# A two-layer transformer kernel: the score operands of the second attention go through a DRAM scratch, and its output is summed before the projection

## The chip, the cores and the metric

The kernel runs on one core of a Trainium2 chip. The core has a matrix engine (TensorE, PE in the profile, with its weight loads shown apart as PEld), a vector engine (DVE), an activation engine (ScalarE, ACT), GpSimd (POOL) and SyncE (SP), whose queue here issues the DMAs. All of them run their own instruction lists in order and wait for one another by semaphores. The metric is the device time of one execution in microseconds.

## What is computed

Two layers. Each normalises its input x, computes an attention s and a gate g = silu(a feed-forward product), and returns x + s * g. The change is in the second layer: its attention has 16 heads of 16 dimensions over sequences of 256 tokens, 8 sequences (batches), and its feed-forward part is a mixture of experts.

```python
def _L1_attn_ref(x, w_qkv, q_norm_w, k_norm_w, w_proj, b_proj):
    qkv = jnp.einsum('bld,ed->ble', x, w_qkv)
    qkv = qkv.reshape(B, L, 3, H, D).transpose(2, 0, 3, 1, 4)
    q, k, v = (qkv[0], qkv[1], qkv[2])
    q = rmsnorm(q, q_norm_w)
    k = rmsnorm(k, k_norm_w)
    scores = jnp.einsum('bhqd,bhkd->bhqk', q, k) * scale
    attn = jax.nn.softmax(scores, axis=-1)
    out = jnp.einsum('bhqk,bhkd->bhqd', attn, v)
    out = out.transpose(0, 2, 1, 3).reshape(B, L, dim)
    return jnp.einsum('bld,ed->ble', out, w_proj) + b_proj
...
x = x + s * g
xn = _layernorm(x, axis=-1)
s = _L1_attn_ref(xn, ...)
g = _silu(_L1_ffn_ref(xn, ...))
return x + s * g
```

All of it is fp32. PE multiplies in a faster format that keeps fewer bits (fp32r), so every operand is split into a hi part (its rounding) and a lo part (the rest), and a product is three: hi x hi, hi x lo, lo x hi (`product`, lines 58 to 60).

## The kernel before

The first layer takes the time to about 890 us. The second is one merged loop, `stage_layer1`, over slots n = -16 to 132, one head per slot: head u of batch b is slot n = 16 b + u. In slot n PE issues the scores of head n + 1, then the items that a planner has put into the slot, then the turn (four transposes of the normalised probabilities) of head n - 1, then the values product of head n - 2. Around it go, for each head: DVE's row maximum (`l_nb`), ACT's exponentials with their sums (`l_pr`), DVE's reciprocal (`l_ri`), GpSimd's normalisation (`l_pr` again), the turn on PE, and its hi part on ACT and lo part on DVE (both `s_wh`). There is one bank for scores, so the scores of a head wait until the exponentials of the head before have been read out of it.

The items are the attention's own jobs, fixed to slots by `attn_jobs`, and the expert work in pieces: `g`, `G`, `u`, `U` (three matmuls of 512 columns each, gate and up products of an expert tile K, 56 tiles in all) and `D0`, `D1` (six of 256 columns, the down product). The planner goes through the slots with a credit: each slot gets SLOT_GOAL - UNIT units, an item costs the units of COST, and expert pieces are added while there is credit. So fewer units for attention jobs, or a higher goal, put expert pieces into earlier slots, and the table alone sets PE's order. The other engines' orders follow from the same table.

The attention's jobs for a batch: Q0, Q1, V (the products of normalised rows and weights), T (transposes), then the S jobs, one in every second slot, eight per batch, one for a pair of heads. The operands of the scores are stacks: for each head 4 x 16 rows, so that hi and lo parts of q stand against hi and lo parts of k in one product over K = 128 rows (two heads, the query operand `zq` being zero for the other head). The stacks are made with tokens on the partitions (`stq`, `stk`), by ACT (`k_hi`, `q_hi`), GpSimd (`q_lo`) and DVE (`k_lo`), 32 instructions of each. An S job turns them on PE (four transposes), and ACT copies them out of PSUM into `zq` and `sk`, three copies.

The values product of four heads fills one bank with 128 rows: per head 16 rows from the hi part of v and 16 from the lo part. After four heads ACT copies the bank (`out_hi`) and DVE takes the rest (`out_lo`), so `ot` has four blocks of 128 rows, in which hi and lo rows stand side by side, and the projection jobs P0, P1 sum them by multiplying over 4 x 128 rows, 12 matmuls of 256 columns.

SP's queue loads the experts' weights (`l_wd`, `s_wl` from wgu_scratch) and the combine rows (`l_cb`, the experts' weights per token, spread over partitions), each as soon as a buffer comes free, in a loop over K.

## Time and profile before

| | us |
|---|---|
| median of 3 runs (lowest, highest) | 1409.71 (1409.17, 1410.26) |
| profiled execution | 1408.91 |
| its span, first to last instruction | 1407.1 |
| busy in the span: PE, DVE, ACT, POOL | 1368.9, 920.9, 820.0, 761.9 |

Busy time is a union of an engine's instructions; matmuls are pipelined, so their listed durations overlap and the step between two starts is the better measure of what one costs. The stage that the change touches is the last third of the span.

### The profile page before, as it was taken

To read this page: it belongs to the slowest core of one execution; us is meant where nothing else is said; L and a number is where in the kernel's file an instruction comes from. 1 tells how busy PE (TensorE), PEld (TensorE's weight loads), DVE (VectorE), ACT (ScalarE), POOL (GpSimd) and SP (SyncE) were. 2 spreads that over 40 slices of the span, in tenths; PEclk is the share of its full clock that TensorE was granted. 3 is DMA by queue.
4 is the path that set the end of the run, shared out by engine and by line. 5 is a ranking of instruction groups with operands and counts; after the bars stand their busy time and mean duration, and the time that the engine had idled before them with its cause. 6 is when DMAs were issued, how large, how long until landed. Compare 5 with 4: busy or idle time off the path is not lost. (4 is left out here: it accounts for less than half of the span.)

```text
span 1407.1 us, 25856 instructions
## 1 busy us (share of the span) xinstructions
PE 1368.9 (97%) x8950; PEld 1221.1 (87%) x8950; DVE 920.9 (65%) x1793; ACT 820.0 (58%) x2172; POOL 761.9 (54%) x757
## 2 busy tenths in 40 slices
PE   9999899999999999999999999899999999999997
PEld 7887798999899989998999888788889888889887
DVE  6655566565656565656665665677777878777764
ACT  5553444554544555445544544378787788778873
POOL 2651433454434454435544443477669677777764
PEclk9999999999999999999999999999999999999999
DMA  5995333334332343223433334144233242342442
GB/s 197 323 330 198 85 91 89 92 80 120 100 94 52 101 130 99 75 75 98 114 86 94 113 75 165 68 122 150 83 98 123 68 150 84 120 120 92 143 122 90
DMA packets 85681, 165.64 MB, mean 118 GB/s; under 512 B 16720, under 2 KB 27664, under 8 KB 83248
## 3 DMA queue, kind: packets, MB, share of 16 engines
q1 hardware_dynamic: 85552, 163.99, 38.3%
q8 instruction: 73, 1.20, 0.4%
q14 instruction: 56, 0.46, 0.1%
HBM read 99.90 MB, written 22.09 MB: 87 GB/s over the span
## 5 line engine op out<-in xcount | busy, mean ns | idle before, releaser
L775 POOL TENSOR_TENSOR a_pr<-a_pr,a_ri 128x512 f32<-128x512 f32 x128 | 133.5, 1043 | 299.1 <-DVE a_ri L955 299.1
L832 ACT ACTIVATE a_pr<-a_score,a_nb 128x256 f32<-128x256 f32 x256 | 119.3, 471 | 266.3 <-DVE a_nb L947 266.3
L1337 POOL TENSOR_TENSOR l_pr<-l_pr,l_ri 128x512 f32<-128x512 f32 x128 | 133.5, 1043 | 119.0 <-DVE l_ri L1714 118.1
L1465 ACT ACTIVATE l_pr<-l_score,l_nb 128x256 f32<-128x256 f32 x256 | 119.2, 472 | 80.8 <-DVE l_nb L1680 80.2
L58 PE MATMUL a_job<-s_xs,s_wh 128*128 128x512 f32 x384 | 153.9, 401 | 1.0 <-PEq L221 1.0
L60 PE MATMUL a_job<-s_xs,s_wl 128*128 128x512 f32 x384 | 151.7, 395 | 0.0
L59 PE MATMUL a_job<-s_xs,s_wh 128*128 128x512 f32 x384 | 151.3, 394 | 0.0
L947 DVE TENSOR_REDUCE a_nb<-a_score 128x2 f32<-128x512 f32 x128 | 88.5, 692 | 85.0 <-PE a_score L1026 83.3
L1680 DVE TENSOR_REDUCE l_nb<-l_score 128x2 f32<-128x512 f32 x128 | 87.5, 684 | 34.0 <-PE l_score L1820 33.4
L960 DVE TENSOR_TENSOR a_pt<-a_turn,a_pt 128x512 fp32r<-128x512 f32 x128 | 87.5, 683 | 24.2 <-ACT a_pt L840 24.2
L1844 PE MATMUL l_out<-s_wh,l_vp 128*128 128x256 f32 x512 | 91.6, 300 | 0.9 <-DVE s_wh L1684 0.9
L58 PE MATMUL l_job<-l_xs,s_wl 128*128 128x512 f32 x224 | 90.6, 405 | 1.7 <-DVE l_ga L1594 1.7
L1684 DVE TENSOR_TENSOR s_wh<-l_turn,s_wh 128x512 fp32r<-128x512 f32 x128 | 87.2, 681 | 5.5 <-ACT s_wh L1473 5.4
L1473 ACT ACTIVATE s_wh<-l_turn 128x512 fp32r<-128x512 f32 x128 | 76.5, 597 | 23.4 <-PE l_turn L1830 23.0
L60 PE MATMUL l_job<-l_xs,s_wl 128*128 128x512 f32 x224 | 88.9, 397 | 0.0
L59 PE MATMUL l_job<-l_xs,s_wl 128*128 128x512 f32 x224 | 88.6, 396 | 0.0
L955 DVE RECIPROCAL a_ri<-a_sm 128x2 f32<-128x2 f32 x128 | 21.2, 166 | 102.3 <-ACT a_pr L832 102.3
L1830 PE MATMUL l_turn<-s_ident,l_pr 128*128 128x128 f32 x512 | 77.9, 275 | 10.5 <-DVE s_wh L1684 9.4
L60 PEld LDWEIGHTS a_job<-s_xs,s_wl 128*128 128x128 f32 x384 | 72.1, 188 | 16.9
L1830 PEld LDWEIGHTS l_turn<-s_ident,l_pr 128*128 128x128 f32 x512 | 59.3, 140 | 28.6 <-issue 13.6
L844 ACT ACTIVATE a_ot<-a_out 128x512 fp32r<-128x512 f32 x64 | 38.8, 606 | 77.8 <-PE a_out L60 76.8
L58 PEld LDWEIGHTS a_job<-s_xs,s_wh 128*128 128x128 f32 x384 | 72.2, 188 | 11.3 <-issue 1.4
(257 smaller groups left out, 4780.3 us busy)
## 6 DMA issues: line engine op xcount, KB each, us to landing
s_wl<-wgu_scratch SPq DMA_DIRECT2D x56, 512.0 KB, 4.8
a_sk<-a_rotk SPq DMA_DIRECT2D x384, 64.0 KB, 2.0
a_sq<-a_rotq SPq DMA_DIRECT2D x256, 64.0 KB, 2.0
s_xs<-xn_scratch SPq DMA_DIRECT2D x14, 1024.0 KB, 5.6
l_wd<-wd_scratch SPq DMA_DIRECT2D x56, 256.0 KB, 2.7
a_raw<-in_w SPq DMA_DIRECT2D x30, 256.0 KB, 3.0
wgu_scratch<-f_split SPq DMA_DIRECT2D x14, 512.0 KB, 4.7
f_praw<-in_moe_w SPq DMA_DIRECT2D x14, 384.0 KB, 4.5
```

What stands on the lines that cost most here:

```text
L58: pe.matmul(out, lh, rh, start=first, stop=False)
L59: pe.matmul(out, lh, rl, start=False, stop=False)
L60: return pe.matmul(out, ll, rh, start=False, stop=last)
L775: pool.tensor_tensor(e, e, ri[:, n % 2, :].unsqueeze(2).broadcast_to([P, 2, SEQ]), ALU.mult)\
L832: i = act.activation(pr[:, n % 2, t, :], PS[n % 2][:, t * SEQ:(t + 1) * SEQ], ACT.Exp, bias=nb[:, n % 2, t:t + 1], accum_out=sm[:, n % 2, ...
L947: dve.tensor_reduce(nb[:, (n + 1) % 2, :], PS[(n + 1) % 2][:, :].rearrange("p (t k) -> p t k", t=2), AX.X, ALU.max, negate=True).then_inc( ...
L960: dve.tensor_tensor(pt[:, n % 2, 1, :], PT[:, :], pt[:, n % 2, 0, :], ALU.subtract).then_inc(S["turn_free"], 1)
L1337: pool.tensor_tensor(e, e, ri[:, n % 3, :].unsqueeze(2).broadcast_to([P, 2, SEQ]), ALU.mult)\
L1465: i = act.activation(pr[:, n % 3, t, :], PS[n % NPS][:, t * SEQ:(t + 1) * SEQ], ACT.Exp, bias=nb[:, n % 3, t:t + 1], accum_out=sm[:, n % 3 ...
L1680: dve.tensor_reduce(nb[:, (n + 1) % 3, :], PS[(n + 1) % NPS][:, :].rearrange("p (t k) -> p t k", t=2), AX.X, ALU.max, negate=True).then_in ...
L1830: i = pe.transpose(PT[:, kc * SEQ + t * P:kc * SEQ + (t + 1) * P], pr[:, n % 3, t, kc * P:(kc + 1) * P], ident[:, :])
L1844: i = pe.matmul(PO[:, 0:SEQ], vp[:, kc, a, e * P:(e + 1) * P], pt[:, n % 2, q, kc * SEQ:(kc + 1) * SEQ], start=(e == 0 and kc == 0 and q = ...
```

## The change

It does four things, all in the second layer.

- The normalised rows of q and k of a batch are turned once, in two X jobs of four transposes each (in slots u = 9 and 11 of the batch before; batch 0 in slots -7 and -5). ACT copies the hi part of the turned rows out of PSUM (`tqk`), DVE takes the lo part. `k_hi`, `q_hi`, `q_lo`, `k_lo` and the S jobs with their evictions go.
- SP writes the turned rows to DRAM scratches in the order of the stacks, eight DMAs for each X job (`store_stack`, in slots u = 10 and 12), and reads the stacks of a pair of heads back into `zq` and `sk` with three DMAs (`load_stack`, in every odd slot, four slots ahead of the pair's first scores). The scores wait for these loads. SP's loop now runs over slots, and a load of expert data stands in the slot in which its buffer comes free.
- The rows of v are laid out so that the hi parts of four heads fill one half of the bank and the lo parts the other. ACT copies the lo half across to the partitions of the hi half (`out_low`), DVE adds the two (`out_sum`). After eight heads ACT and DVE split the 128 summed rows into hi and lo parts (`out_hi`, `out_lo`), and the projection runs over 2 x 128 rows.
- The planner's cost of a P job goes from 12 to 6 units and SLOT_GOAL from 30.6 to 28.35.

The rest of the diff renames semaphores, makes the weights of the projection two blocks instead of four, and adds the scratches.

```diff
-VG, VSTRIDE, VBLK = 4, 160, 640
+VG, VB, VSTRIDE, VBLK = 4, 2, 144, 576
+VHALF = VG * D1
...
-    T, Q, V, S_, P_, LOG, CMB, GU, DH = 4, 12, 12, 4, 12, 20, 4, 12, 6
+    T, Q, V, S_, P_, LOG, CMB, GU, DH = 4, 12, 12, 4, 6, 20, 4, 12, 6
...
-    UNIT, SLOT_GOAL, EARLY_GOAL = 10, 30.6, 14
+    UNIT, SLOT_GOAL, EARLY_GOAL = 10, 28.35, 14
...
-        m, r = divmod(n + 4, H1)
-        if r % 2 == 0 and 0 <= m < BATCH:
-            jobs.append((f"S{r // 2}", m))
+        if b + 1 < BATCH and u in (9, 11):
+            jobs.append((f"X{u // 2 - 4}", b + 1))
...
+                def store_stack(m, half):
+                    wait_free(sp, (f"X{half}", m))
+                    heads = slice(8 * half, 8 * half + 8)
+                    for part, to, places in ((0, qs_dram, ((0, 2), (1, 3))), (1, ks_dram, ((0, 1), (2, 3)))):
+                        for low in range(2):
+                            for place in places[low]:
+                                sp.dma_start(to[m % 2, heads, place], tqk[:, half, low, part, :].bitcast(F32)).then_inc(tqk_out[half], 16)
+
+                def load_stack(pair):
+                    m, p = divmod(pair, H1 // 2)
+                    r = pair % NSTK
+                    if p % 4 == 0:
+                        sp.wait_ge(tqk_out[p // 4], 16 * 8 * (m + 1))
+                    if pair >= NSTK:
+                        sp.wait_ge(S["score_full"], 2 * (pair - NSTK) + 2)
+                    for h in range(2):
+                        sp.dma_start(zq[64 * h:64 * h + 64, r, h, :].bitcast(F32),
+                                     qs_dram[m % 2, 2 * p + h].rearrange("c d n -> (c d) n")).then_inc(zq_in[r], 16)
+                    sp.dma_start(sk[:, r, :].bitcast(F32), ks_dram[m % 2, 2 * p:2 * p + 2].rearrange("h c d n -> (h c d) n")).then_inc(sk_in[r], 16)
...
+                for n in SLOTS:
+                    b, u = divmod(n, H1)
+                    if b + 1 < BATCH and u in (10, 12):
+                        store_stack(b + 1, u // 2 - 5)
+                    pair = (n + 5) // 2
+                    if n % 2 and 0 <= pair < N // 2:
+                        load_stack(pair)
+                    for K in LOAD_AT[n]:
+                        load_experts(K)
+                    for K in range(2, L):
+                        if LOAD_GU[K] == n:
+                            load_gu(K)
...
-                    elif name[0] == "S":
...
-                        for h in range(2):
-                            act.activation(zq[64 * h:64 * h + 64, r, h, :], bank[64 * h:64 * h + 64, 0:SEQ], ACT.Copy)
-                        act.activation(sk[:, r, :], bank[:, SEQ:2 * SEQ], ACT.Copy).then_inc(free_of(item), 1)
+                    elif name[0] == "X":
+                        half = int(name[1])
                         wait_full(act, item)
+                        if m >= 1:
+                            act.wait_ge(tqk_out[half], 16 * 8 * m)
+                        act.activation(tqk[:, half, 0].rearrange("p r n -> p (r n)"), bank[:, :], ACT.Copy).then_inc(S["turned_hi"], 1)
...
-                def out_hi(g):
+                def out_low(g):
+                    here, there = VHALF * (g % 2), VHALF * (1 - g % 2)
                     act.wait_ge(S["pv_done"], 4 * g + 4)
...
+                    act.activation(ol[here:here + VHALF, :], PO[there:there + VHALF, 0:SEQ], ACT.Copy).then_inc(S["out_low"], 1)
+
+                def out_hi(k):
+                    act.wait_ge(S["out_free"], 2 * k + 2)
+                    if k >= VB:
+                        wait_full(act, ("P1", k // VB - 1))
+                    act.activation(ot[:, 0, k % VB, :], os[:, k % VB, :], ACT.Copy).then_inc(S["out_hi"], 1)
...
-                def out_lo(g):
-                    dve.wait_ge(S["out_hi"], g + 1)
-                    dve.tensor_tensor(ot[:, 1, g % VG, :], PO[:, 0:SEQ], ot[:, 0, g % VG, :], ALU.subtract).then_inc(S["out_free"], 1)
+                def out_sum(g):
+                    here = VHALF * (g % 2)
+                    dve.wait_ge(S["out_low"], g + 1)
+                    if g >= 4:
+                        dve.wait_ge(S["out_lo"], (g - 4) // 2 + 1)
+                    dve.tensor_tensor(os[here:here + VHALF, g // 2 % VB, :], PO[here:here + VHALF, 0:SEQ], ol[here:here + VHALF, :], ALU.add)\
+                       .then_inc(S["out_free"], 1)
+
+                def out_lo(k):
+                    dve.wait_ge(S["out_hi"], k + 1)
+                    dve.tensor_tensor(ot[:, 1, k % VB, :], os[:, k % VB, :], ot[:, 0, k % VB, :], ALU.subtract).then_inc(S["out_lo"], 1)
...
-                        pe.wait_ge(S["out_free"], VG * (m + 1))
-                        for a in range(VG):
+                        pe.wait_ge(S["out_lo"], VB * (m + 1))
+                        for a in range(VB):
...
                     if u % 2 == 0:
-                        wait_free(pe, (f"S{u // 2}", m))
+                        pe.wait_ge(zq_in[r], 16 * 2 * (n // 2 // NSTK + 1))
+                        pe.wait_ge(sk_in[r], 16 * (n // 2 // NSTK + 1))
```

Three places in the orders of instructions. First PE: a slot of before with an S job, from the scores on (L1820 are the scores, L58 to L60 an expert piece, L1773 the S job, L1742 to L1744 a down piece).

```order
L1820 MATMUL l_score<-l_sk,l_zq 128x256 x2
L58 MATMUL l_job<-l_xs,s_wl 128x512
L59 MATMUL l_job<-l_xs,s_wl 128x512
L60 MATMUL l_job<-l_xs,s_wl 128x512
L1773 MATMUL l_job<-s_ident,l_stq 128x128 x2
L1773 MATMUL l_job<-s_ident,l_stk 128x128 x2
L1742 MATMUL l_down<-l_wd,l_hid 128x256
L1743 MATMUL l_down<-l_wd,l_hid 128x256
L1744 MATMUL l_down<-l_wd,l_hid 128x256
L1742 MATMUL l_down<-l_wd,l_hid 128x256
L1743 MATMUL l_down<-l_wd,l_hid 128x256
L1744 MATMUL l_down<-l_wd,l_hid 128x256
```

In the changed kernel the slot that has the X1 job of the same batch, to the next slot's scores (L1787 is the X job, L59 to L61 an expert piece, L1844 the turn, L1858 the values).

```order
L1834 MATMUL l_score<-l_sk,l_zq 128x256 x2
L1787 MATMUL l_job<-s_ident,l_qk 128x128 x4
L59 MATMUL l_job<-l_xs,s_wl 128x512
L60 MATMUL l_job<-l_xs,s_wl 128x512
L61 MATMUL l_job<-l_xs,s_wl 128x512
L59 MATMUL l_job<-l_xs,s_wl 128x512
L60 MATMUL l_job<-l_xs,s_wl 128x512
L61 MATMUL l_job<-l_xs,s_wl 128x512
L1844 MATMUL l_turn<-s_ident,l_pr 128x128 x4
L1858 MATMUL l_out<-s_wh,l_vp 128x256 x4
L1834 MATMUL l_score<-l_sk,l_zq 128x256 x2
```

The four transposes now read the rows themselves (`l_qk`) and stand in two slots of sixteen; the slots between have scores, expert pieces, turn and values alone.

Second SP's queue, before, in the middle of a batch (L1242 and L1247 are the weights of an expert tile, L1262 the combine rows).

```order
L1242 DMA s_wl<-wgu_scratch 128x1024
L1247 DMA l_wd<-wd_scratch 128x512
L1262 DMA l_cb<-ct_scratch 64x512 x2
L1242 DMA s_wl<-wgu_scratch 128x1024
L1247 DMA l_wd<-wd_scratch 128x512
L1262 DMA l_cb<-ct_scratch 112x512
L1262 DMA l_cb<-ct_scratch 16x512
L1242 DMA s_wl<-wgu_scratch 128x1024
```

In the changed kernel, slots u = 9 to 12 of a batch (L1272 are the stores, L1282 and L1284 the loads of a pair's stacks, L1243, L1248, L1263 the loads of before).

```order
L1263 DMA l_cb<-ct_scratch 64x512 x2
L1243 DMA s_wl<-wgu_scratch 128x1024
L1272 DMA qs_scratch<-l_tqk 8x16x256 x4
L1272 DMA ks_scratch<-l_tqk 8x16x256 x4
L1282 DMA l_zq<-qs_scratch 64x256 x2
L1284 DMA l_sk<-ks_scratch 128x256
L1243 DMA s_wl<-wgu_scratch 128x1024
L1272 DMA qs_scratch<-l_tqk 8x16x256 x4
L1272 DMA ks_scratch<-l_tqk 8x16x256 x4
L1248 DMA l_wd<-wd_scratch 128x512
L1263 DMA l_cb<-ct_scratch 112x512
L1263 DMA l_cb<-ct_scratch 16x512
```

Sixteen stores and a pair's loads have come between the loads of expert weights and combine rows.

Third DVE in the slot u = 2 after a batch's first: before, the last low part of the attention's output stands right behind the low part of the turn (L1680 is a row maximum, L1684 the low part of a turn, L1655 `out_lo`, L1602 to L1605 row norms, L1714 the reciprocal).

```order
L1680 TENSOR_REDUCE l_nb<-l_score 128x2
L1684 TENSOR_TENSOR s_wh<-l_turn,s_wh 128x512
L1655 TENSOR_TENSOR l_ot<-l_out,l_ot 128x256
L1602 TENSOR_REDUCE l_ss<-l_sqr 128x64
L1603 TENSOR_SCALAR l_ss<-l_ss 128x64
L1605 TENSOR_SCALAR l_rq<-l_ss 128x64
L1598 TENSOR_TENSOR l_ga<-l_ga,l_job 128x512
L1714 RECIPROCAL l_ri<-l_sm 128x2
```

In the changed kernel the sum `out_sum` (L1664) has that place, and `out_lo` (L1669) stands behind the row norms and the reciprocal (L1726), two places ahead of the next row maximum (L1694).

```order
L1694 TENSOR_REDUCE l_nb<-l_score 128x2
L1698 TENSOR_TENSOR s_wh<-l_turn,s_wh 128x512
L1664 TENSOR_TENSOR l_os<-l_out,l_ol 64x256
L1614 TENSOR_REDUCE l_ss<-l_sqr 128x64
L1615 TENSOR_SCALAR l_ss<-l_ss 128x64
L1617 TENSOR_SCALAR l_rq<-l_ss 128x64
L1726 RECIPROCAL l_ri<-l_sm 128x2
L1669 TENSOR_TENSOR l_ot<-l_os,l_ot 128x256
L1610 TENSOR_TENSOR l_ga<-l_ga,l_job 128x512
```

So the operand of the projection jobs, which PE has in the slots u = 3 and 4, is finished later in DVE's slot.

## Rows read from the trace of the kernel before

**Rows 1.** The page, busy time of each engine over the span.

```profile
PE 1368.9 (97%) x8950; PEld 1221.1 (87%) x8950; DVE 920.9 (65%) x1793; ACT 820.0 (58%) x2172; POOL 761.9 (54%) x757
```

**Rows 2.** Stretches of time: length, busy time of each engine, granted clock, DMA.

```profile
core 0: us, PE busy (x) PEld busy (x) DVE busy (x) ACT busy (x) POOL busy (x), PEclk, DMA share, GB/s
...
921.60:1383.80 462.20, 449.02 (x3137) 404.40 (x3138) 349.34 (x739) 358.79 (x1051) 339.75 (x414) 1.00 0.37 115
1000.30:1051.40 51.10, 46.76 (x314) 41.38 (x313) 40.79 (x92) 40.49 (x117) 31.18 (x34) 1.00 0.28 89
1250.50:1303.40 52.90, 52.90 (x377) 48.27 (x377) 36.72 (x74) 43.23 (x127) 39.84 (x52) 1.00 0.38 121
```

**Rows 3.** Waits of the second layer: total us, times, longest.

```profile
ACT l_pr L1465 <- DVE l_nb L1680: 80.2, 106, 2.1
...
PE l_turn L1830 <- DVE s_wh L1684: 9.4, 14, 1.3
...
PEld l_turn L1830 <- POOL l_pr L1337: 7.6, 9, 1.7
```

**Rows 4.** Timeline of PE, two neighbouring slots: start us, us, instruction.

```profile
1261.14 0.39 PE L1820 MATMUL l_score<-l_sk,l_zq 128*128 128x256 f32 x2
...
1262.06 0.38 PE L1773 MATMUL l_job<-s_ident,l_stq 128*128 128x128 f32 x2
...
1264.80 0.40 PE L1820 MATMUL l_score<-l_sk,l_zq 128*128 128x256 f32 x2
...
1265.74 0.28 PE L1742 MATMUL l_down<-l_wd,l_hid 128*128 128x256 f32 x1
...
1266.32 0.28 PE L1744 MATMUL l_down<-l_wd,l_hid 128*128 128x256 f32 x1
...
1268.04 0.28 PE L1820 MATMUL l_score<-l_sk,l_zq 128*128 128x256 f32 x1
```

**Rows 5.** Groups by shape: count, busy us, mean ns, idle before.

```profile
L1420 ACT ACTIVATE l_zq<-l_job 64x256 fp32r<-64x256 f32 x128 | 48.0, 375 | 1.5 <-PE l_job L1773 0.5
...
L1773 PE MATMUL l_job<-s_ident,l_stk 128*128 128x128 f32 x128 | 24.4, 272 | 0.0
...
L1619 DVE TENSOR_TENSOR l_stk<-l_qk,l_stk 128x256 fp32r<-128x256 f32 x32 | 23.1, 762 | 0.0
...
L58 PE MATMUL l_job<-s_wl,l_ot 128*128 128x256 f32 x64 | 18.4, 287 | 0.0
...
L1655 DVE TENSOR_TENSOR l_ot<-l_out,l_ot 128x256 fp32r<-128x256 f32 x32 | 13.2, 414 | 1.2 <-ACT l_ot L1479 1.2
```

**Rows 6.** Timeline of one slot at 1019 us, rows of DVE, ACT, PE.

```profile
1020.77 0.73 DVE L1582 SCALAR_TENSOR_TENSOR l_ga<-l_gt,l_gz 128x512 f32<-128x512 f32 x1 [2.57 <-ACT l_gt L1439]
...
1021.09 0.74 ACT L1449 ACTIVATE l_stk<-l_qk 128x256 fp32r<-128x256 f32 x2
...
1022.85 0.63 PE L1830 MATMUL l_turn<-s_ident,l_pr 128*128 128x128 f32 x4 [0.84 <-DVE s_wh L1684]
```

**Rows 7.** Timeline of SP's queue in the first layer, loads of 64 KB.

```profile
418.46 3.70 SPq L689 DMA_DIRECT2D a_sk<-a_rotk  x6
```

**Rows 8.** The page, DMA issues: count, KB each, us to landing.

```profile
a_sk<-a_rotk SPq DMA_DIRECT2D x384, 64.0 KB, 2.0
...
l_wd<-wd_scratch SPq DMA_DIRECT2D x56, 256.0 KB, 2.7
```

**Rows 9.** Stores to a DRAM scratch: issue ns, shortest, median and longest.

```profile
L249 SPq DMA_DIRECT2D xn_scratch<-s_xs x4: 339/876/1222, 12.8 to 94.4; - x4
```

**Rows 10.** Two stretches at the head of the second layer, columns of rows 2.

```profile
897.00:900.20 3.20, 3.05 (x26) 3.08 (x27) 2.70 (x6) 0.00 (x0) 2.14 (x5) 0.99 0.00 0
900.20:903.60 3.40, 3.40 (x11) 2.75 (x10) 2.80 (x12) 0.88 (x3) 2.52 (x8) 0.50 0.00 0
```

**Rows 11.** Timeline of the head, rows of POOL, SP and PE.

```profile
911.54 1.66 POOL L1317 TENSOR_TENSOR l_stq<-l_qk,l_stq 128x256 fp32r<-128x256 f32 x2 [0.18 <-ACT l_stq L1457]
...
918.35 0.36 SPq L1262 DMA_DIRECT2D l_cb<-ct_scratch  x1
...
918.69 0.39 PE L1820 MATMUL l_score<-l_sk,l_zq 128*128 128x256 f32 x2
...
922.86 1.30 POOL L1344 TENSOR_TENSOR l_ga<-l_ga,l_cb 128x512 f32<-128x512 f32 x1
```

More of the change, by code:

```diff
@@ L750, in _ @@
                     sp.dma_start(l1.w[:, :, c].bitcast(F32), w1_dram[c]).then_inc(l1.w_in, 16)
-                for i in range(2):
-                    sp.dma_start(l1.wp[:, :, 2 * i:2 * i + 2].bitcast(F32).rearrange("p s a d -> p s (a d)"), wp_dram[i]).then_inc(l1.w_in, 16)
+                sp.dma_start(l1.wp.bitcast(F32).rearrange("p s a d -> p s (a d)"), wp_dram[0]).then_inc(l1.w_in, 16)
                 sp.wait_ge(S["job_full"], JOB["k3", NST - 1] + 1)
@@ L1077, in _, with stage_layer1 @@
                 rest(PS[(N - 2) % 2], 9)
-def stage_layer1(nc, sh, l1, wgu_dram, wd_dram, ct_dram, out):
+def stage_layer1(nc, sh, l1, wgu_dram, wd_dram, ct_dram, qs_dram, ks_dram, out):
     N = BATCH * H1
@@ L1133, in stage_layer1 @@
     JOB = {item: i for i, item in enumerate(ORDER)}
+    LOAD_SLOT, at = {}, SLOTS[0]
+    for K in range(L + 1):
+        s, k = divmod(K, MT)
+        at = max(at, AT["D1", K - 1 - ND] if K > ND else SLOTS[0], AT["C", s] if k == NSH + 1 and s < NSTEP else SLOTS[0])
+        LOAD_SLOT[K] = at
+    LOAD_GU = {K: AT["U", K - NGU] if K >= NGU else SLOTS[0] for K in range(L)}
+    LOAD_AT = {n: [K for K in LOAD_SLOT if LOAD_SLOT[K] == n] for n in SLOTS}
     U_AT = {n: [K for K in range(L) if AT["U", K] == n] for n in SLOTS}
@@ L1196, in stage_layer1 @@
         gu_in = l1.gu_in
+        zq_in, sk_in = ([n_.sem(f"{s}_in{i}") for i in range(NSTK)] for s in ("zq", "sk"))
+        tqk_out = [n_.sem(f"tqk_out{i}") for i in range(2)]
         d_in, cb_in = ([n_.sem(f"{s}_in{i}") for i in range(3)] for s in ("d", "cb"))
@@ L1223, in tokens @@
             return slice(at, at + P)
-        def heads(t, part, half):
-            at = part * D + half * P
-            return qk[:, t, at:at + P].rearrange("p (h d) -> p h d", d=D1).unsqueeze(2).broadcast_to([P, 8, 2, D1])
-        def half_of(rows, t, half):
-            return rows[:, t, 8 * half:8 * half + 8]
         def wait_merged(engine, s):
@@ L1272, in store, with load_experts @@
                                      x1[:, s * TT + 2 * i:s * TT + 2 * i + 2, :]).then_inc(S["stored"], 16)
-                for K in range(L + 1):
-                    if 2 <= K < L:
-                        load_gu(K)
+                def load_experts(K):
                     if K >= 1:
@@ L1313, in weigh @@
                         .then_inc(S["weighted"], 1)
-                def q_lo(m, half, t):
-                    pool.wait_ge(S["q_hi"], 4 * m + 2 * half + t + 1)
-                    pool.tensor_tensor(half_of(stq, t, half)[:, :, 1::2, :].bitcast(F32R), heads(t, 0, half),
-                                       half_of(stq, t, half)[:, :, 0::2, :], ALU.subtract).then_inc(S["q_lo"], 1)
                 def spread(m, a):
@@ L1442, in job_out @@
                             act.activation(gt[:, m % 2, :], bank[:, :], ACT.Tanh, scale=0.5).then_inc(S["tanh_ready"], 1)
-                def k_hi(m, half):
-                    act.wait_ge(S["scaled"], m + 1)
-                    if m >= 1:
-                        wait_full(act, (f"S{4 * half + 3}", m - 1))
-                    for t in range(TB):
-                        act.activation(half_of(stk, t, half)[:, :, 0:2, :].bitcast(F32R), heads(t, 1, half), ACT.Copy)\
-                           .then_inc(S["k_hi"], 1)
-                def q_hi(m, half):
-                    act.wait_ge(S["weighted"], m + 1)
-                    if m >= 1:
-                        wait_full(act, (f"S{4 * half + 3}", m - 1))
-                    for t in range(TB):
-                        act.activation(half_of(stq, t, half)[:, :, 0::2, :].bitcast(F32R), heads(t, 0, half), ACT.Copy)\
-                           .then_inc(S["q_hi"], 1)
                 def exps(n):
@@ L1614, in scale_rows @@
                                       rq[:, :].unsqueeze(2).broadcast_to([P, 4 * H1, D1]), ALU.mult).then_inc(S["scaled"], 1)
-                def k_lo(m, half):
-                    for t in range(TB):
-                        dve.wait_ge(S["k_hi"], 4 * m + 2 * half + t + 1)
-                        dve.tensor_tensor(half_of(stk, t, half)[:, :, 2:4, :].bitcast(F32R), heads(t, 1, half),
-                                          half_of(stk, t, half)[:, :, 0:2, :], ALU.subtract).then_inc(S["k_lo"], 1)
                 def rows(ap):
@@ L1714, in _ @@
                         dve.reciprocal(ri[:, (n + 1) % 3, :], sm[:, (n + 1) % 3, :]).then_inc(S["sum_inv"], 1)
+                    if n >= 10 and (n - 10) % 8 == 0 and (n - 10) // 8 < VB * BATCH:
+                        out_lo((n - 10) // 8)
                     for item in second:
@@ L1851, in _ @@
                 do_item(("T", 0))
-                pe.wait_ge(l1.w_in, 64)
+                pe.wait_ge(l1.w_in, 48)
                 rest(PO, 5)
@@ L1877, in program @@
     ct = nc.dram_tensor("ct_scratch", [2, E, STEP], F32, kind="Internal").ap()
+    qs = nc.dram_tensor("qs_scratch", [2, H1, 4, D1, SEQ], F32, kind="Internal").ap()
+    ks = nc.dram_tensor("ks_scratch", [2, H1, 4, D1, SEQ], F32, kind="Internal").ap()
     with ExitStack() as ctx:
@@ L1884, in program @@
             stage_attention0(nc, a, sh, s0, l1, xn0, g0, w1, wp, wgu)
-        stage_layer1(nc, sh, l1, wgu, wd, ct, out)
+        stage_layer1(nc, sh, l1, wgu, wd, ct, qs, ks, out)
 def tile_weights(gate, up, down):
@@ L1901, in proj_rows @@
     import numpy as np
-    rows = [[(VG * a + p // (2 * D1)) * D1 + p % D1 for p in range(P)] for a in range(VG)]
+    rows = [[(2 * VG * j + p // D1) * D1 + p % D1 for p in range(P)] for j in range(VB)]
     return np.concatenate([w[r] for r in rows], axis=1)
```

64 lines of the change are left out of this document (27 added, 37 removed).

## Prediction

> **What bounds the kernel now.** I read the busy line of the page first: PE works in 97% of the span, DVE in 65%, ACT in 58% [rows 1]. That is an average over two layers, and the change is in the second one, so the next view was the busy time by stretches. From 921.6 to 1383.8 us, where 126 heads run with the experts' products between them, PE is busy 449.0 of 462.2 us at the full granted clock, DVE 349.3 and ACT 358.8 [rows 2]. So 13.2 us of that stretch are not PE's own work, and they are not spread evenly: from 1250.5 to 1303.4 PE has no idle time at all, from 1000.3 to 1051.4 it has 4.3 us [rows 2]. The third view is the waits. The long one (ACT's exponential behind DVE's row maximum, 80.2 us) is ACT's idle time and costs nothing while PE goes on; PE's own largest is its turn of the probabilities behind DVE's low part of the head before, 9.4 us in 14 times [rows 3]. The reader should see: work taken from PE here is nearly all time, work taken from ACT is time only in the few slots where a chain over ACT and DVE ends last.
>
> The timeline of two neighbouring slots shows what an instruction is worth on PE. A slot with an S job takes from 1261.14 to 1264.80, 3.66 us; the next one, alike but without it, to 1268.04, 3.24 us [rows 4]. So an S job (four fp32 transposes) costs 0.42 us. Six matmuls of 256 columns start 0.116 us apart (1265.74 to 1266.32 over five steps) [rows 4]; their listed durations of 0.28 overlap and are not to be added.
>
> **Removed from PE.** 64 S jobs become 16 X jobs of four transposes each: 48 x 0.42 = 20.2 us. The projection multiplies over 2 blocks of 128 rows rather than 4, so 6 of 12 matmuls go in each of 16 P jobs: the three lines hold 64 matmuls each [rows 5], 192, of which 96 go: 96 x 0.116 = 11.1 us. Together 31.3 us, all in the second layer. The values, turns, scores and expert products stay. The planner's goal falls from 30.6 to 28.35 units, so expert pieces move to earlier slots to fill the room; that is what turns the saving into shorter slots (most come to 3.24 us [rows 4]) instead of gaps, and itself costs nothing.
>
> **The other engines.** ACT loses the evictions of S (48.0 us, and half as much for the sk tile) and the hi copies into the stacks; it gains 32 low-half copies of 64x256 at about 0.375 us, the price of the same shape in the S eviction [rows 5], 12 us, and 16 X copies of 128x512. DVE loses 32 low parts of k at 0.762 us mean (24.4 us) and gains 16 X subtractions, at most twice the 0.414 us of a subtraction of half the size from PSUM [rows 5], 13 us, and per eight heads one operation more, 16 x 0.41 = 7 us. So DVE's sum falls a little, ACT's much, and GpSimd loses its low parts of q. No engine but PE is near the span by its sum. I price these edits at nothing on the sum, because PE's 449 us cover them. Without that cover, where the chain decides, they are a gain: in the slot at 1019 PE waited 0.84 us for DVE, whose work of that slot began after 2.57 us of waiting for ACT, and ACT put 0.74 us of k's hi copies between [rows 6]. Those copies go.
>
> One new low part is unlike the old: out_lo now reads two SBUF tiles, where the old one read PSUM. The traces show that kind of difference: k's low part from two SBUF tiles takes 0.762 us on average, the old out_lo of equal size from PSUM 0.414 [rows 5]. So 16 out_lo may take 0.35 us more, 6 us of DVE time that PE covers, against 32 of the slow kind that go. The Trainium skill, page "SBUF — State Buffer", section "Who interferes with whom", says that a DVE instruction with two SBUF inputs and a GpSimd instruction reading SBUF shut each other out for a whole instruction; the trace agrees in that mean. By that rule the change halves the exposed instructions; by the row of equal size alone the DVE sum would differ by those 6 us, and the time by nothing.
>
> **Added on the SP queue.** Before each batch SP stores the turned rows in two bursts of eight DMAs of 128 KB, and loads three per pair of heads, 64 pairs. No row shows a store of this shape. Below: 0.34 us of issue, the fastest of four stores to xn_scratch; above: 1.22, the slowest of them [rows 9]. In between, six 64 KB loads took 3.70 us back to back, 0.62 each [rows 7], nearest in kind and size; I take that. A burst is then 5.0 us, a pair's loads 1.9. A pair is loaded four slots (13 us) ahead of its scores, and lands in about 2.0 us [rows 8], so a queue that is one burst late still delivers. Behind the stores in the same queue stand the experts' weights and the combine rows cb. The first cb was issued at 918.35 and used at 922.86, 4.5 us later [rows 11], so a burst in front of it can be felt. GpSimd's combine then runs late, behind it the normalisation of a head, and PE's turn waits for that. From 0 to 1 us a burst, 16 bursts; I take 0.2, 3 us.
>
> **New waits.** P0 waits for out_lo, which now comes behind three operations on row norms and a reciprocal in DVE's slot. Bounds: nothing, and 0.8 us in each of 8 batches; nearer nothing, since PE has scores and expert pieces ahead of it. I take 2 us in all. At the head the first scores stand at 918.69; the change puts X0 where the first q low part ran, at 911.54 to 913.20 [rows 11]. From about 912.5: eight stores of 0.62 us, 2.0 to land, three loads of 0.62, 2.0 to land, give 923.4, 4.7 us late. With 0.34 for each issue it is 920.2, 1.5 us late. I take 3; nothing stands behind PE's wait that could run instead, and if the clock falls over it, as it stood at 0.50 (1.2 of 2.4 GHz) from 900.2 to 903.6 after 3.2 us with only 26 matmuls [rows 10], 1.7 us more, half of those 3.4. The Trainium skill, page "DMA: Bandwidth & Descriptors", section "Why a DMA increments its semaphore by 16 and not by 1", says that the slowest dimension of both sides sets how many of 16 DMA engines share a transfer; with 8 heads in front it would be 8 here. By that the 128 KB would load each engine like 256 KB over all, which lands in 2.7 instead of 2.0 us [rows 8], and the head would be 0.7 us later; no run here shows it yet.
>
> At the end, the last P0 and P1 are short (counted above) but their operand passes four operations instead of two (0.8 us more); PE's keep-busy products cover most of that, and I set it to nothing, plus or minus 1.
>
> **Sum.** Against the profiled execution's 1408.9 us (its span of 1407.1 and 1.8 around it, 0.8 under the median of the runs): 1408.9 - 31.3 + 3 (head) + 3 (SP bursts) + 2 (out_lo) = 1385.6 us. PE's present 13.2 us of waiting are taken to stay: shorter slots leave the chains less cover, but the chains lose ACT and DVE work too.
>
> **Rivals.** (1) The chains shrink with the work: the new waits cost nothing and half of the 13.2 us of idle time goes, since k's hi copies [rows 6] are out of ACT's way: 1408.9 - 31.3 + 3 - 6.6 = 1374. For it: the slot at 1019; against: DVE's sum hardly falls, and its 349 us are a larger share of a shorter stretch (349 of about 433, 81% instead of 76%). (2) The SP bursts and DVE's chain take back more: 0.75 us more in each of 16 bursts, 12 us, gives 1397.6. For it: cb's 4.5 us and a queue without a second one; against: most loads are issued well ahead. (3) Nothing is gained: the slots end at the chains, whatever PE has to do. ACT's 80.2 us behind DVE would be the sign, but there is a stretch of 52.9 us without any idle time of PE [rows 2], so this needs every slot to change its limit: about 1409. (4) Slower: the stores issue at 1.22 us each. Two bursts are then 19.5 us in about four slots (13 us), in which SP also has about 3.7 us of pair loads and 3 of expert loads: it falls 13 us behind, the weights with it, and PE waits some 8 us in each of 7 batches: 1385.6 + 56 = 1442. It decides the sign from 23 / 7 = 3.3 us a batch. Against it: only one row is that long, and the queue stores 1 MB there, not 128 KB.
>
> **How the numbers follow.** A measurement of this kernel can tell about 0.2%, 2.8 us, from no change. The forecast's case, 1380 to 1391, has 0.50; rival 1, down to 1372, 0.20; rival 2, 1391 to 1406, 0.22; rival 3 0.03; rival 4 0.05. Faster 0.92, same 0.03, slower 0.05. With the head at 1.5 and the other two unknown costs at nothing the sum is 1379.1, and only rival 1 lies below; with the head at 6.4, the bursts at 16 and out_lo at 6.4 it is 1406.4. The range from 1374 to 1400 leaves out 0.04 below, about 0.06 of rival 2 and the last two rivals, 0.18 in all.
>
> **What would show it.** In the profile after: S transposes gone, X groups of 16 x 4; the projection lines halved; slots without other jobs at 3.24 us; PE still over 95% busy in the second layer; one wait of some us at the first scores, ended by the sk or zq DMA. Wrong: PE waits at scores for DMAs all along, store issues over 1 us, or the turn's wait for DVE or GpSimd well above 9.4 and 7.6 us [rows 3]; or slots that stay at 3.6 us although PE has 3.24 us of work in them.

## The result, and the profile after

The changed kernel takes 1445.38 us (median of 4 runs, 1444.11 to 1449.18) against 1409.44: the ratio is 1.0252, with an interval from 1.0238 to 1.0266. It is slower by 36 us; the forecast was 1385.6, in a range from 1374 to 1400. The busy line of the page, and the span with its granted clock:

```profile
PE 1351.5 (94%) x8662; PEld 1201.0 (83%) x8662; DVE 915.3 (63%) x1793; ACT 754.9 (52%) x1947; POOL 743.2 (51%) x724
...
core 0: 1444.7 us, clock 0.981
```

Each figure of the busy line is below the one before [rows 1], and the span is 37.6 us longer. By stretches, from the row maximum of the first head to that of the last: 464.4 us before (919.8 to 1384.2), 497.4 after (926.5 to 1423.9). So 33.0 us lie among the heads, 6.7 at the head of the layer, and its tail is 2.1 us shorter. The stretch of the heads, and four pieces of one hole in it (columns of [rows 2]):

```profile
926.50:1423.90 497.40, 433.98 (x2871) 385.48 (x2871) 344.92 (x742) 299.04 (x843) 325.49 (x386) 0.96 0.58 173
...
992.00:996.00 4.00, 0.26 (x3) 0.05 (x1) 0.00 (x0) 0.00 (x0) 0.00 (x0) 0.84 0.82 245
996.00:1000.00 4.00, 0.00 (x0) 0.00 (x0) 0.00 (x0) 1.07 (x3) 2.36 (x3) 0.50 0.94 289
1000.00:1004.00 4.00, 1.88 (x9) 1.92 (x10) 2.56 (x5) 2.15 (x7) 3.53 (x6) 0.50 1.03 293
1004.00:1008.00 4.00, 4.00 (x23) 3.52 (x22) 3.26 (x10) 2.65 (x7) 0.99 (x2) 0.88 0.38 115
```

PE now has 63 us in which it does nothing, where it had 13.2 [rows 2], and its clock falls to the lower level (1.2 of 2.4 GHz) behind a hole. The waits of the layer (total us, times, longest), those of SP's queue last:

```profile
POOL l_ga L1371 <- DMA l_cb<-ct_scratch: 49.4, 10, 11.2
PE l_turn L1844 <- DVE s_wh L1698: 44.4, 29, 9.9
...
PEld l_turn L1844 <- POOL l_pr L1364: 23.1, 23, 2.8
...
PE l_score L1834 <- DMA l_sk<-ks_scratch: 14.0, 3, 8.1
...
SPq L1282 <- DMA ks_scratch<-l_tqk: 22.5, 8, 4.3
```

The wait that was not there before is GpSimd's for the combine rows cb, 49.4 us; the turn's wait for DVE (9.4 before [rows 3]) stands behind it. It and the turn's wait for GpSimd (23.1, before 7.6) are the sign of being wrong that the prediction named. Followed through the hole at 992, SP's queue first (L1272 stores, L1282 and L1284 a pair's loads, L1263 cb):

```profile
974.78 2.51 SPq L1272 DMA_DIRECT2D qs_scratch<-l_tqk  x4
977.34 2.72 SPq L1272 DMA_DIRECT2D ks_scratch<-l_tqk  x4
983.92 1.13 SPq L1282 DMA_DIRECT2D l_zq<-qs_scratch  x2
985.09 0.59 SPq L1284 DMA_DIRECT2D l_sk<-ks_scratch  x1
985.72 0.43 SPq L1243 DMA_DIRECT2D s_wl<-wgu_scratch  x1
986.20 2.52 SPq L1272 DMA_DIRECT2D qs_scratch<-l_tqk  x4
988.75 2.98 SPq L1272 DMA_DIRECT2D ks_scratch<-l_tqk  x4
991.78 0.69 SPq L1248 DMA_DIRECT2D l_wd<-wd_scratch  x1
992.51 1.00 SPq L1263 DMA_DIRECT2D l_cb<-ct_scratch  x2
```

Then GpSimd, which had been free since 986.5, and PE:

```profile
997.64 1.26 POOL L1371 TENSOR_TENSOR l_ga<-l_ga,l_cb 128x512 f32<-128x512 f32 x1 [11.16 <-DMA l_cb<-ct_scratch]
998.86 1.04 POOL L1364 TENSOR_TENSOR l_pr<-l_pr,l_ri 128x512 f32<-128x512 f32 x1
...
1002.12 0.66 PE L1844 MATMUL l_turn<-s_ident,l_pr 128*128 128x128 f32 x2 [9.85 <-DVE s_wh L1698]
```

The two bursts and what stands between them hold SP from 974.78 to 991.78, 17.0 us: stores 5.3, then 3.9 us in which SP itself waits until they have landed, a pair's loads and a weight load 2.2, stores 5.6. The cb rows issue at 992.5, GpSimd has them 5 us later, and PE stands for 9.85 us. Summed over the layer SP is not short of time: it still stands 110.3 us (L1248) and 65.3 us (L1243) until a product frees a weight buffer. It is late by the block, not by the sum. At the head of the layer the same happens twice, before the first and the third head's scores:

```profile
925.66 0.77 PE L1834 MATMUL l_score<-l_sk,l_zq 128*128 128x256 f32 x2 [4.93 <-DMA l_sk<-ks_scratch]
...
940.56 0.76 PE L1834 MATMUL l_score<-l_sk,l_zq 128*128 128x256 f32 x2 [8.11 <-DMA l_sk<-ks_scratch]
```

### The profile page after: what moved, and what is told of

It reads as the page before. It is cut to its first block and busy times, and to the rows that moved or that the text cites. A ratio compares the mean times of both kernels' runs of the same rounds, so it can differ in the third digit from the quotient of the medians.

```text
span 1444.7 us, 25243 instructions
## 1 busy us (share of the span) xinstructions
PE 1351.5 (94%) x8662; PEld 1201.0 (83%) x8662; DVE 915.3 (63%) x1793; ACT 754.9 (52%) x1947; POOL 743.2 (51%) x724
## 5 line engine op out<-in xcount | busy, mean ns | idle before, releaser
L59 PE MATMUL a_job<-s_xs,s_wh 128*128 128x512 f32 x384 | 153.9, 401 | 1.0 <-PEq L222 1.0
L61 PE MATMUL a_job<-s_xs,s_wl 128*128 128x512 f32 x384 | 151.7, 395 | 0.0
L60 PE MATMUL a_job<-s_xs,s_wh 128*128 128x512 f32 x384 | 151.3, 394 | 0.0
L1844 PE MATMUL l_turn<-s_ident,l_pr 128*128 128x128 f32 x512 | 80.0, 280 | 46.9 <-DVE s_wh L1698 44.4
L1844 PEld LDWEIGHTS l_turn<-s_ident,l_pr 128*128 128x128 f32 x512 | 60.0, 143 | 67.0 <-issue 37.1
L1694 DVE TENSOR_REDUCE l_nb<-l_score 128x2 f32<-128x512 f32 x128 | 87.4, 683 | 40.2 <-PE l_score L1834 39.8
L1858 PE MATMUL l_out<-s_wh,l_vp 128*128 128x256 f32 x512 | 93.9, 306 | 0.0
L59 PE MATMUL l_job<-l_xs,s_wl 128*128 128x512 f32 x224 | 90.3, 403 | 2.2 <-DVE l_ga L1606 2.2
L60 PE MATMUL l_job<-l_xs,s_wl 128*128 128x512 f32 x224 | 89.5, 400 | 0.0
L61 PE MATMUL l_job<-l_xs,s_wl 128*128 128x512 f32 x224 | 89.5, 399 | 0.0
L61 PEld LDWEIGHTS a_job<-s_xs,s_wl 128*128 128x128 f32 x384 | 72.1, 188 | 16.9
L1371 POOL TENSOR_TENSOR l_ga<-l_ga,l_cb 128x512 f32<-128x512 f32 x44 | 57.1, 1298 | 51.1 <-DMA l_cb<-ct_scratch 49.4
L59 PEld LDWEIGHTS a_job<-s_xs,s_wh 128*128 128x128 f32 x384 | 72.2, 188 | 11.3 <-issue 1.4
```

Source lines behind the costliest of these rows:

```text
L59: pe.matmul(out, lh, rh, start=first, stop=False)
L60: pe.matmul(out, lh, rl, start=False, stop=False)
L61: return pe.matmul(out, ll, rh, start=False, stop=last)
L1694: dve.tensor_reduce(nb[:, (n + 1) % 3, :], PS[(n + 1) % NPS][:, :].rearrange("p (t k) -> p t k", t=2), AX.X, ALU.max, negate=True).then_in ...
L1844: i = pe.transpose(PT[:, kc * SEQ + t * P:kc * SEQ + (t + 1) * P], pr[:, n % 3, t, kc * P:(kc + 1) * P], ident[:, :])
L1858: i = pe.matmul(PO[:, 0:SEQ], vp[:, kc, a, e * P:(e + 1) * P], pt[:, n % 2, q, kc * SEQ:(kc + 1) * SEQ], start=(e == 0 and kc == 0 and q = ...
```

## The experiments

**The two halves of the change, alone.** The first kept the S jobs and took only the summed output and the short projection; the second the reverse.

```diff
 # projection alone, against the kernel before
-    T, Q, V, S_, P_, LOG, CMB, GU, DH = 4, 12, 12, 4, 12, 20, 4, 12, 6
-    UNIT, SLOT_GOAL, EARLY_GOAL = 10, 30.6, 14
+    T, Q, V, S_, P_, LOG, CMB, GU, DH = 4, 12, 12, 4, 6, 20, 4, 12, 6
+    UNIT, SLOT_GOAL, EARLY_GOAL = 10, 29.85, 14
...
 # stacks alone, against the changed kernel
-    T, Q, V, S_, P_, LOG, CMB, GU, DH = 4, 12, 12, 4, 6, 20, 4, 12, 6
-    UNIT, SLOT_GOAL, EARLY_GOAL = 10, 28.35, 14
+    T, Q, V, S_, P_, LOG, CMB, GU, DH = 4, 12, 12, 4, 12, 20, 4, 12, 6
+    UNIT, SLOT_GOAL, EARLY_GOAL = 10, 29.1, 14
```

> Only the second half of the change: both parts of the attention's output summed on the way out, projection over 256 rows, S jobs and SP's loop as before, the planner's goal at 29.85 units. Queue theory (SP's stores and the wait for them hold up the combine rows cb, and all else follows): this half has no stores, so it gains its 96 matmuls, 11.1 us, about 1399. Rival 'short slots' (the chains over ACT, DVE and GpSimd lose their cover when PE has less to do): a part of the 11.1 us at most, 1403 to 1409. Rival 'traffic': as the queue theory.

> Only the first half: rows turned once, stacks by way of the DRAM scratch, S jobs gone, output and projection as before, goal 29.1. Queue theory: all of the loss is here, and the projection's 11 us are missing: about 1452 to 1460. Rival 'traffic': the same. Rival 'short slots': PE has 11 us more work as cover than in the changed kernel, so no slower than it, 1440 to 1447.

The projection alone gave 1410.21 us, ratio 1.0004 (0.9995 to 1.0014): none of its 11 us. The stacks alone gave 1453.08. So the loss is all in the scratch, as the queue theory had it, but the queue theory was wrong on the other half. The stretch of [rows 2] in the projection's kernel:

```profile
921.60:1383.80 462.20, 439.84 (x3032) 392.93 (x3031) 358.37 (x750) 364.95 (x1062) 343.71 (x412) 1.00 0.37 115
```

PE is busy 9.2 us less than before and idle 9.2 us more; DVE and ACT have 9 and 6 us more. So PE's time was freed where something else ends the slots. Whether that is the work that was there before or the 9 us that DVE now has more, this run does not separate.

**Order in SP's list.** Two kernels moved loads and nothing else.

```diff
 # experts' loads first in each slot
+                    for K in LOAD_AT[n]:
+                        load_experts(K)
...
                     if b + 1 < BATCH and u in (10, 12):
                         store_stack(b + 1, u // 2 - 5)
...
 # cb early: cb leaves load_experts, and has a slot of its own
-                    if K >= 1 and not is_shared(K - 1):
-                        load_cb(K - 1)
+    CB_SLOT = {K: max(LOAD_SLOT[K // MT * MT + NSH + 1], AT["U", ROUTED[j - NCB]] + 2 if j >= NCB else SLOTS[0]) for j, K in enumerate(ROUTED)}
```

> The changed kernel, but in each slot SP issues the experts' loads first, then the stores, then the pair's loads; same DMAs, same bytes. Queue theory: cb loads no longer stand behind a burst of their own slot, the 49 us that GpSimd waits for cb fall to under 20 and the time to 1400 to 1425. Rival 'traffic': no change, 1440 to 1448. Rival 'short slots': no change.

> The changed kernel with the same stores, loads, bytes and buffers, but each cb load stands in SP's list up to two slots earlier, as soon as the combine of three routed tiles before has freed its buffer, instead of behind the weights of its tile. Queue theory with cb as the victim: GpSimd's wait for cb (49 us) falls under 10 and the time to 1400 to 1420. Rival 'pair loads' (the waits for cb only hide that zq, sk or the weights would be as late): cb's wait goes, waits at scores or expert pieces take its place, 1435 to 1447. Rival 'traffic': no change.

The first gave 1452.40 us, a miss: the wait for cb fell only to 35.6 us, and the scores' wait for the stacks rose from 14.0 to 28.8. The experts' loads wait for a product late in PE's slot (SP waits 140.7 us for it, where it was 110.3), and the stores and pairs behind them came later by that. The second gave 1427.69, 17.7 us better with the same transfers, between the ranges of the queue theory and of the rival 'pair loads'. The wait for cb fell to 8.3 us, once, but the rival is half right as well:

```profile
PE l_score L1837 <- DMA l_sk<-ks_scratch: 27.1, 7, 9.9
```

A queue that is 17 us behind makes late whatever stands last in it.

**Fewer stores.** The same bytes in four DMAs of 256 KB (rows of all 8 heads in each, the row order inside a head changed alike for q and k), and then the same with four small stores more.

```diff
-                        for low in range(2):
-                            for place in places[low]:
-                                sp.dma_start(to[m % 2, heads, place], tqk[:, half, low, part, :].bitcast(F32)).then_inc(tqk_out[half], 16)
+                    for i in range(2):
+                        sp.dma_start(qs_dram[m % 2, half, :, i], tqk[:, half, :, 0, :].bitcast(F32)).then_inc(tqk_out[half], 16)
+                    for i in range(2):
+                        sp.dma_start(ks_dram[m % 2, half, :, :, i], tqk[:, half, :, 1, :].bitcast(F32)).then_inc(tqk_out[half], 16)
...
 # and in the second kernel
+                    for i in range(4):
+                        sp.dma_start(small_dram[m % 2, half, i], tqk[:, half, 0, 0, 0:16].bitcast(F32)).then_inc(tqk_out[half], 16)
```

> The changed kernel with the same bytes stored in four DMAs of 256 KB for each X job instead of eight of 128 KB, rows of a head interleaved differently in the scratch, loads of the same sizes. Queue theory: a burst takes 2.4 instead of 5.0 us of SP's issue and its landing starts earlier, so SP is about 6 us less late per batch: 1405 to 1425. Rival 'traffic': same bytes, so 1440 to 1448. Rival 'short slots': no change.

> The kernel with four stores of 256 KB for each X job, and four stores of 8 KB behind them, to a scratch that nobody reads: as many issues as in the changed kernel, the bytes of the version with four. Queue theory by number of issues: 4 x 0.6 us more per burst, so most of the 29 us that the four stores gave back is lost again, 1430 to 1445. Rival 'shape' (the four were better because each large store spreads over more DMA engines and lands sooner): 1416 to 1422.

Four stores: 1416.30 us, 29 us better. With the small ones: 1426.49, 10 of the 29 lost again, less than was expected. SP's queue at the first batch with four stores:

```profile
967.18 0.95 SPq L1269 DMA_DIRECT2D qs_scratch<-l_tqk  x2
968.17 1.96 SPq L1271 DMA_DIRECT2D ks_scratch<-l_tqk  x2
974.53 1.13 SPq L1282 DMA_DIRECT2D l_zq<-qs_scratch  x2
...
976.81 0.94 SPq L1269 DMA_DIRECT2D qs_scratch<-l_tqk  x2
977.80 1.74 SPq L1271 DMA_DIRECT2D ks_scratch<-l_tqk  x2
979.58 0.87 SPq L1248 DMA_DIRECT2D l_wd<-wd_scratch  x1
```

From the first store to the first load behind the second burst it is 12.4 us here against 17.0. The bytes are the same, so traffic as such is not what made the change slow. 64 issues fewer gave 29 us, 64 small ones more took 10. The block tells why the two differ: on average over the eight batches it is 17.3 us long with eight stores, 11.8 with four and 15.2 with the small ones. These cost SP nearly as much issue (0.50 us in the median), but SP waits less for landing (10.3 us in 6 waits, against 22.5 in 8). So the issues and the landing both count. Whether the larger stores also spread over the DMA engines in another way, no run shows.

**Another queue.** The stores from ScalarE's queue, eight or four of them.

```diff
-                                sp.dma_start(to[m % 2, heads, place], tqk[:, half, low, part, :].bitcast(F32)).then_inc(tqk_out[half], 16)
+                                act.dma_start(to[m % 2, heads, place], tqk[:, half, low, part, :].bitcast(F32)).then_inc(tqk_out[half], 16)
...
                     if n in SUM_AT:
                         y_tanh(SUM_AT[n])
+                    if b + 1 < BATCH and u in (10, 12):
+                        store_stack(b + 1, u // 2 - 5)
```

> The changed kernel with its eight stores issued on ScalarE's queue instead of SP's, nothing else. Queue theory: SP's bursts go, but ScalarE stands 5 us in two slots of 16 with the exponentials of the next head behind it: 1395 to 1415. Rival 'traffic' or 'short slots': 1440 to 1448.

> The version with four stores, but issued on ScalarE's queue at the end of its slot, behind the rounding copies. Same DMAs, same bytes; SP's queue has loads alone. Queue theory: SP no longer comes late, cb's wait goes under 8 us and the time to 1388 to 1402; ScalarE pays about 2 us of issue in two slots of 16. Rival 'traffic': as the version with four stores on SP, 1413 to 1420. Rival 'short slots': as well.

Eight: 1473.87 us, four: 1416.61. Both miss. ScalarE's timeline in the kernel with eight:

```profile
981.97 2.47 ACTq L1497 DMA_DIRECT2D qs_scratch<-l_tqk  x4
984.47 3.88 ACTq L1497 DMA_DIRECT2D ks_scratch<-l_tqk  x4
988.74 0.60 ACT L1469 ACTIVATE s_wh<-l_turn 128x512 fp32r<-128x512 f32 x1 [6.18 <-issue]
```

An issue holds the engine that makes it for 0.6 us and more, and ScalarE has the turn of a head behind it, where SP had loads with some slots to spare. The stores are no cheaper there, only worse placed. Nor was SP relieved of them: it stood 75.1 us (eight) and 49.6 us (four) in its own queue until they had landed, where it was 22.5 and 22.2 with the stores in its own list. The four cost the same from either queue (1416.61 and 1416.30).

**Both cures, and what is left.** Four stores and the early cb together; then three variants of it: the row norms of q and k over 4 of 16 elements, the projection's half taken back, and the pairs' loads three slots ahead instead of four.

```diff
 # short norm
-                    own(dve.tensor_reduce(ss[:, :], sqr[:, :, :].rearrange("p t (g d) -> p (t g) d", d=D1), AX.X, ALU.add))
+                    own(dve.tensor_reduce(ss[:, :], sqr[:, :, :].rearrange("p t (g d) -> p (t g) d", d=D1)[:, :, 0:4], AX.X, ALU.add))
...
 # lead of three
-                    pair = (n + 5) // 2
-                    if n % 2 and 0 <= pair < N // 2:
+                    pair = (n + 4) // 2
+                    if n % 2 == 0 and 0 <= pair < N // 2:
```

> Both single cures of the queue together: four stores of 256 KB for each X job, and cb loads as soon as their buffer is free. The four stores alone gave 1416, the early cb alone 1428 from 1445. Queue theory: what is left of the waits for cb (23 us) and at scores (27 us) goes, 1400 to 1408, and no batch of heads has a slot over 8 us except at the head. If the two cure the same microseconds only: 1413 to 1418.

> The version with both cures, and the sum of squares in the row norms of q and k taken over 4 of 16 elements (12 of 16 are left out), which takes about 0.8 us off one DVE instruction in slot 2 of each batch; nothing else changes. Theory 'short slots' (with the queue cured, DVE's order ends the slots 1 to 5 of a batch, since PE has 3.2 us of work there and DVE over 4): 0.5 to 0.8 us in each of 8 batches, 4 to 7 us below the version with both cures. Queue theory alone: no difference over 2 us.

> The version with both cures but with output and projection as in the kernel before (K of 128 rows for four heads, 12 matmuls in a P job, goal 29.1): what the projection's half is worth when the queue does not decide. By PE's work it would be 11 us slower than with it. Theory 'short slots': PE's 11 us lie in slots that DVE ends, so 0 to 6 us slower only.

> The version with both cures, with the loads of a pair three slots ahead of its scores instead of four, and ahead of the stores in a slot, so that SP need not stand still until a batch's first stores have landed (22 us in 7 to 8 waits so far). Queue theory: SP's wait for landing falls under 5 us, the time 2 to 8 us below the version with both cures, unless the shorter lead makes zq and sk late: then waits at scores rise over 10 us and it is slower.

Both cures: 1407.57 us, ratio 0.9989 (0.9980 to 0.9998), within what can be told from the kernel before. GpSimd waits 5.0 us for cb, once, and in five batches (the second, and the fourth to the seventh) no slot is over 5.1 us; these five take some 57 us each all the same, with PE busy in 53 to 54 of them. The short norm gives a part of the reason: 1399.47, 8.1 us less (the runs of either version scatter by 4 us). The norm runs once at the head and in one slot of each of seven batches, and each time it takes 0.80 us less. Of the 9.4 us between the two traced executions, 4.6 are its slots in the second to the seventh batch (0.6 to 0.8 each). 2.4 lie ahead of the first row maximum and 2.1 in the first batch, where the waits at the head move as well. DVE's timeline of the slot in the version with both cures, from one row maximum to the next:

```profile
1174.16 0.67 DVE L1699 TENSOR_REDUCE l_nb<-l_score 128x2 f32<-128x512 f32 x1
1174.74 0.68 DVE L1703 TENSOR_TENSOR s_wh<-l_turn,s_wh 128x512 fp32r<-128x512 f32 x1
1175.45 0.43 DVE L1669 TENSOR_TENSOR l_os<-l_out,l_ol 64x256 f32<-64x256 f32 x1
1175.91 1.22 DVE L1619 TENSOR_REDUCE l_ss<-l_sqr 128x64 f32<-128x1024 f32 x1
...
1177.63 0.75 DVE L1611 SCALAR_TENSOR_TENSOR l_ga<-l_job,s_bias,l_ga 128x512 f32<-128x512 f32 x1
1178.29 0.15 DVE L1731 RECIPROCAL l_ri<-l_sm 128x2 f32<-128x2 f32 x1
1178.37 0.40 DVE L1674 TENSOR_TENSOR l_ot<-l_os,l_ot 128x256 fp32r<-128x256 f32 x1
1178.69 0.68 DVE L1699 TENSOR_REDUCE l_nb<-l_score 128x2 f32<-128x512 f32 x1
```

And with the short norm:

```profile
1167.39 0.67 DVE L1699 TENSOR_REDUCE l_nb<-l_score 128x2 f32<-128x512 f32 x1
...
1169.15 0.42 DVE L1619 TENSOR_REDUCE l_ss<-l_sqr 128x64 f32<-128x256 f32 x1
...
1171.12 0.68 DVE L1699 TENSOR_REDUCE l_nb<-l_score 128x2 f32<-128x512 f32 x1
```

4.53 us, with no idle time shown on DVE, become 3.73: the slot is as long as DVE's list. Taking the projection's half back cost 2.0 us (1409.57) of PE's 11, which fits that. The shorter lead gave 1410.70, no gain: the wait for landing fell from 22.1 to 12.5 us, the waits at scores rose from 10.1 to 12.5.

**The head of the layer, and the clock.** The version with both cures, with the stores of X1 two slots later; and this with 14 filler products ahead of the first scores.

```diff
-                    if b + 1 < BATCH and u in (10, 12):
-                        store_stack(b + 1, u // 2 - 5)
+                    if b + 1 < BATCH and u in (10, 14):
+                        store_stack(b + 1, (u - 10) // 4)
...
 # and in the second kernel
+                    if n == -1:
+                        rest(PO, 14)
```

> The version with both cures (four stores, early cb), with the four stores of X1 two slots later, behind the loads of the next pair. Queue theory: at the head the second pair's loads no longer stand behind these stores and the 10 us between the second and the third head fall to 4 to 6, in the other batches the bursts lie further apart: 1399 to 1405. If the head only waits for DMA latency: 1406 to 1409.

> The same with 14 products of 512 columns (3.2 us, results unused) ahead of PE's first scores, where it stood still for 3.1 us. Clock theory: the granted clock stays at full over the first slots, where it was 0.5 to 0.6 for some 4 us behind that wait, so 1 to 3 us less although PE does more. If the clock falls through something else: no change, or up to 1 us more.

The first: 1401.14 us, ratio 0.9933 (0.9918 to 0.9948), faster than both kernels; the time between the second and the third head's maxima fell from 10.0 to 6.3 us. The second: 1403.68 (0.9940 to 0.9968), no gain. Its stretches around the first scores, columns of [rows 2]:

```profile
921.00:925.00 4.00, 2.86 (x15) 2.14 (x14) 0.67 (x1) 0.00 (x0) 0.38 (x1) 1.00 0.44 135
925.00:929.00 4.00, 3.70 (x20) 2.75 (x19) 2.92 (x11) 2.53 (x9) 1.17 (x2) 1.00 0.68 181
929.00:933.00 4.00, 0.00 (x0) 0.00 (x0) 1.39 (x3) 1.11 (x2) 3.35 (x3) 0.88 1.01 318
933.00:937.00 4.00, 3.47 (x10) 2.92 (x11) 0.69 (x1) 1.13 (x5) 0.00 (x0) 0.50 1.01 331
```

The clock stayed up over the first scores, as the clock theory had it. But the second pair's loads land when they land: PE ran ahead, stood still from 929 on, and the clock fell there.

## Why the prediction was wrong, step by step

**PE's savings: right, and not the bound.** The instructions went as counted (64 X transposes, 32 projection matmuls in each of three lines). In the version with the late X1, PE is busy 426.0 us from first to last head, against 450.8 before, 25 us less even with some half-clock time in it (before, then late X1):

```profile
919.80:1384.20 464.40, 450.81 (x3149) 405.73 (x3149) 350.65 (x742) 360.21 (x1056) 341.34 (x418) 1.00 0.38 115
...
926.50:1381.40 454.90, 426.03 (x2872) 379.46 (x2872) 346.36 (x743) 298.41 (x843) 325.67 (x386) 0.99 0.62 189
```

**The step that failed: "From 0 to 1 us a burst, 16 bursts; I take 0.2, 3 us."** The price of a store was right: 0.62 and 0.57 us, and the pair's loads 0.6.

```profile
L1272 SPq DMA_DIRECT2D qs_scratch<-l_tqk x64: 570/616/1648, 913.2 to 1365.2; - x64
L1272 SPq DMA_DIRECT2D ks_scratch<-l_tqk x64: 570/571/1048, 915.9 to 1368.7; - x64
```

What was left out is that SP stands still in its own queue until the stores have landed (22.5 us in 8 waits), so that the two bursts of a batch are one block of 17 us. The paragraph held one burst against the pairs' lead of 13 us, and of the 4.5 us of cb, which it names, it said only that a burst "can be felt"; the block was held against neither. The landing was too short as well: the pairs' loads took 3.8 us (zq) and 3.7 us (sk) in the median and up to 7.7, not 2.0. Curing the queue (four stores, early cb, later X1) took the time from first to last head from 497.4 to 454.9 us. That is 42.5 us for the term that was set at 3, with what the clock lost behind the holes in it.

**The head.** Forecast 3 us late, below the 4.7 that its own steps gave; the first scores came 6.97 us late (918.69 to 925.66). The stores began 0.7 us later than taken, took 0.7 us more, and landed 3.2 us after the last issue instead of 2.0. A second wait of 8.1 us was not in the sum: the second pair's loads stood behind the stores of X1.

**"PE's present 13.2 us of waiting are taken to stay": wrong.** With the queue cured, first to last head takes 454.9 us where 464.4 less PE's 31.3 would be 433; PE stands still in 28.9 us of it, where it was 13.6. The short norm shows DVE's list as the end of one slot in six of the batches. The null of the projection alone fits that without any scratch, and 2.0 us for the projection's half fits it with the cured one. That DVE ends the other long slots at the start of a batch is read from the trace, not tested slot by slot: with both cures it is busy for 95 to 97% of each of the 14 slots over 4.4 us among heads 1 to 7 of the second to the seventh batch. Three such slots later in a batch have it busy for 40 to 82%, and what ends them is open, as is the rest of the 22 us. The sentence that the edits on DVE cost nothing "because PE's 449 us cover them" held for sums; in a slot PE had 3.2 us and DVE 4.5.

**The rivals.** Rival 4, slower, gave 1442, close to the time. Its mechanism held in kind (SP falls behind, and PE's idle time grows by 50 us) but not its condition: it asked for 1.22 us an issue, and 0.62 is enough. So it is partly luck that its time is within 4 us. Its chance of 0.05 was too low, since the block could have been added up from the same rows: 5.0 + 2.0 to land + 1.9 + 5.0 is 14 us. Rival 2 was the same mechanism with the price too small. Rival 3, that the slots end at the chains, has a part in the time that stays when the queue is cured.

**Small terms.** The X subtraction takes 688 ns, under the bound of 828. out_lo, with both inputs in SBUF, takes 521 ns on average, between the 414 of the old one from PSUM and the 762 of k's low part [rows 5]. The mean hides two cases: 13 of the 16 take 402 to 425 ns, and only the three that began while a GpSimd product was running take 526, 1114 and 1414, each ending 0.28 us after that product. This agrees with the rule of the Trainium skill, page "SBUF — State Buffer", section "Who interferes with whom", that the prediction draws on; the time shows nothing of it. P0 waited for out_lo for 4.0 us in 6 times, 2 were taken.

```profile
L1572 DVE TENSOR_TENSOR l_tqk<-l_job,l_tqk 128x512 fp32r<-128x512 f32 x16 | 11.0, 688 | 8.5 <-ACT l_tqk L1443 8.5
...
L59 PE MATMUL l_job<-s_wl,l_ot 128*128 128x256 f32 x32 | 9.7, 303 | 4.3 <-DVE l_ot L1669 4.0 <-DVE l_ga L1600 0.3
L1669 DVE TENSOR_TENSOR l_ot<-l_os,l_ot 128x256 fp32r<-128x256 f32 x16 | 8.3, 521 | 1.1 <-ACT l_ot L1490 1.1
```
